# Selective scan stage: softplus, output and down products spread over the states, and GpSimd makes the product with C for three of the sixteen states from rows in SBUF

## The chip, the core and the metric

One core of a Trainium2 chip runs the whole program in one launch. The metric is device time in microseconds (us). The kernel before took 1541.23 us (median of 3 runs, 1536.33 to 1543.85).

## The reference, cut to what matters

A tokenizer (convolutions, a wavelet packet transform, layer norm) turns 32 images into 49 tokens each; with a class token and 32 text tokens that is a sequence of S = 82 rows of D = 192 for each of the 32 images. Then come a layer norm and a Mamba block with a gated FFN, then self-attention, then a routed feed-forward layer with 8 experts, two of them for each token. The change lies in the Mamba block alone:

```
xdbl = z @ W_xproj.T;  dt_in, Bm, Cm = split(xdbl, [96, 112])
dt   = softplus(dt_in @ W_dt.T + b_dt)          # (S, 384)
A    = -exp(A_log)                              # (384, 16)
h_t  = exp(dt_t * A) * h_(t-1) + (dt_t * z_t) * Bm_t     # for each of 16 states
y    = sum over states of h * Cm  + D_skip * z
x1   = x + y @ W_out.T;   out = x1 + FFN(rmsnorm(x1))
```

## The kernel before, in words

The block works in 8 rounds of G = 4 images, so N = 4 * 82 = 328 columns; the 384 inner channels are NI = 3 tiles of 128 partitions, and a tile of one state is 128 x 984. Within a round the code steps through the 16 states. Every engine runs the same skeleton in program order, `turn(i, par, s)`: its part of the scan for state s (`step`), a piece of the round behind (`post`, round i-1: output product, RMS norm, gated FFN, down product, sum into H) and a piece of the round ahead (`pre`, round i+1: transposes, gate and input products, x projection, softplus). TensorE and ScalarE do `post` and `pre` first and `step` last (`side_first`), VectorE and GpSimd do `step` first. Rounds 1 to 6 have all three parts, round 0 has no `post`, round 7 no `pre`.

What each engine does for one state:

- GpSimd: Bx = dtz * B (`inputs`), three states ahead, ring of 4.
- ScalarE: the decays exp(dt * A) into PSUM (`decays`), two states ahead in program order, but each half waits until the scan of the state before has read that half of the bank.
- VectorE: the scan in two halves (`scan`), from PSUM and Bx into hs, ring of 4; then the product hs * C in place (line 1230).
- TensorE: `spread_c`, a matmul with a one-hot matrix that spreads the C row of a state over 128 partitions of PSUM, two banks in turn; and `add_y`, two f32 matmuls with the identity that add the product to y in PSUM. The round's y is read from PSUM by VectorE (`drain`) in state 0 of the next round.

All products of `pre` and `post` share two PSUM banks (6 and 7) in turn. The list `SIDE_TILES` fixes that order, and `free(name)` makes TensorE wait until the tile two places earlier has been read; for RT1 that tile is O1, which is free once VectorE has made the second half of x1:

```
SIDE_TILES = [("O0", 0, s_x1, 2, 1), ("O1", 0, s_x1, 2, 2), ("RT0", 1, s_hT, 2, 1), ("RT1", 1, s_hT, 2, 2),
              ("RG0", 1, s_z, 3, 1), ("RI0", 1, s_z, 3, 1), ("RG1", 1, s_z, 3, 2), ("RI1", 1, s_z, 3, 2),
              ...
```

Places in the round: state 1, products O0 and O1 and both halves of x1 on VectorE; state 2, transposes RT0, RT1 and on ScalarE hT; states 3 to 5, gate and input products RGm, RIm, tanh on ScalarE, z on VectorE; state 6, x projection, the copy Bs of the B rows, which SyncE writes to DRAM and reads back spread over 128 partitions (Bb); state 7, the remainder terms of C in bf16; states 8 to 10, softplus; states 10 to 13, the FFN products and `th`, `av` on VectorE; state 14, down products N0, N1 and both halves of H.

Softplus is max(x,0) + log(1+exp(-|x|)), plus a rounding term of 1+u. ScalarE makes rl = relu, ax = abs, u = exp(-ax), ax = 1+u, lnw = Ln(1+u), ax = ax-1; GpSimd makes ax = u-ax, ax += lnw, dt = rl+ax (state 10) and dtz = dt*z (state 11).

## Time and profile before

| | us |
|---|---|
| median of 3 runs | 1541.23 |
| the profiled execution, its own time | 1542.03 |
| its span, first to last instruction | 1540.2 |
| TensorE busy, of the span | 1253.2 |
| VectorE | 1045.4 |
| ScalarE | 708.6 |
| GpSimd | 755.4 |
| scan stage, first scan to last product with C | 303.1 to 839.3 |

PE is TensorE, PEld its weight loads, DVE VectorE, ACT ScalarE, POOL GpSimd, SP SyncE. Busy time alone doesn't say what a change is worth. In this kernel the reader looks at one round of some 70 us, sees which engine has idle time there, and what ended it (in brackets at the end of a timeline row: idle time before it, and the instruction waited for).

### The profile page before, as it was taken

To read this page: it belongs to the slowest core of one execution; us is meant where nothing else is said; L and a number is where in the kernel's file an instruction comes from. 1 tells how busy PE (TensorE), PEld (TensorE's weight loads), DVE (VectorE), ACT (ScalarE), POOL (GpSimd) and SP (SyncE) were. 2 spreads that over 40 slices of the span, in tenths; PEclk is the share of its full clock that TensorE was granted. 3 is DMA by queue.
4 is the path that set the end of the run, shared out by engine and by line. 5 is a ranking of instruction groups with operands and counts; after the bars stand their busy time and mean duration, and the time that the engine had idled before them with its cause. 6 is when DMAs were issued, how large, how long until landed. Compare 5 with 4: busy or idle time off the path is not lost. (4 is left out here: it accounts for less than half of the span.)

```text
span 1540.2 us, 19619 instructions
## 1 busy us (share of the span) xinstructions
PE 1253.2 (81%) x5818; PEld 829.1 (54%) x5819; DVE 1045.4 (68%) x1960; ACT 708.6 (46%) x1486; POOL 755.4 (49%) x492
## 2 busy tenths in 40 slices
PE   6796746297898989898878899888898259999996
PEld 4342323143455545555444678777777237777775
DVE  3699787899888989789898566776766403333332
ACT  1147522576757677585853345443432012222221
POOL 2028963568767686757775301333345712222222
PEclk9697657699999999999999999997987569999998
DMA  5100100440404033040500011121211112222221
GB/s 161 53 1 0 28 8 27 154 137 9 132 1 132 30 101 107 25 131 0 154 7 0 2 48 48 50 64 49 67 26 25 40 47 38 35 37 37 35 37 21
DMA packets 71130, 80.89 MB, mean 53 GB/s; under 512 B 13231, under 2 KB 62918, under 8 KB 70970
## 3 DMA queue, kind: packets, MB, share of 16 engines
q1 hardware_dynamic: 51778, 68.50, 14.2%
q0 software_dynamic: 17152, 9.24, 4.4%
q10 hardware_dynamic: 2136, 2.37, 0.5%
q8 instruction: 32, 0.52, 0.1%
q14 instruction: 32, 0.25, 0.1%
HBM read 48.74 MB, written 30.01 MB: 51 GB/s over the span
## 5 line engine op out<-in xcount | busy, mean ns | idle before, releaser
L1333 POOL TENSOR_TENSOR Bx<-dtz,Bb 128x984 f32<-128x984 f32 x128 | 288.9, 2278 | 53.9 <-DVE hs L1220 53.9
L1220 DVE TENSOR_TENSOR_SCAN hs<-ps,Bx 128x492 f32<-128x492 f32 x256 | 287.6, 1164 | 30.4 <-ACT ps L1094 25.4
L1094 ACT ACTIVATE ps<-dt,A 128x324 f32<-128x324 f32 (+1 forms) x512 | 214.1, 454 | 106.3 <-DVE hs L1220 104.8
L954 PE MATMUL ps<-hs,b_id 128*128 128x492 f32 x512 | 243.4, 598 | 11.6 <-DVE y L1188 9.1
L2046 POOL DMA_INDIRECT out<-yt,dest x48 | 74.1, 1543 | 222.2 <-DVE yt L2033 216.8
L1230 DVE TENSOR_TENSOR hs<-hs,ps 128x984 f32<-128x984 f32 x128 | 150.2, 1174 | 2.6
L954 PEld LDWEIGHTS ps<-hs,b_id 128*128 128x128 f32 x512 | 94.3, 197 | 87.7 <-issue 82.3
L1927 PE MATMUL e_ps<-W,xT 97*128 (+1 forms) x384 | 139.9, 507 | 1.8 <-ACT xT L1981 1.0
L2019 DVE COPY hT__9516<-e_ps 128x768 f32<-128x768 f32 x48 | 46.0, 957 | 132.2 <-PE e_ps L1936 131.8
L1946 PE MATMUL e_ps<-W,hT__9516 128*128 x576 | 109.2, 327 | 0.8 <-DVE yb L2027 0.8
L1831 POOL TENSOR_TENSOR c_x<-c_x,bro 82x192 f32<-82x192 f32 x32 | 19.7, 614 | 182.2 <-DVE c_x L1677 181.7
L1987 ACT ACTIVATE hb<-e_ps 128x768 f32<-128x768 f32 x48 | 38.9, 811 | 145.7 <-PE e_ps L1927 145.7
L1822 POOL DMA_INDIRECT buckets<-XS,c_slot x64 | 91.2, 1425 | 24.9 <-issue 19.1
L1927 PEld LDWEIGHTS e_ps<-W,xT 97*128 97x128 f32 (+1 forms) x384 | 70.6, 194 | 56.1 <-issue 18.8
L920 PE MATMUL ps<-hfT,wug 96*128 96x328 f32 x256 | 80.7, 461 | 22.9 <-DVE av L1205 22.1
L1946 PEld LDWEIGHTS e_ps<-W,hT__9516 128*128 128x128 f32 x576 | 91.4, 190 | 1.4 <-issue 1.4
L492 POOL TENSOR_TENSOR DF<-DF,prod 96x441 f32<-96x441 f32 x84 | 87.6, 1043 | 6.6
L939 PE MATMUL ps<-P,sel 96*128 96x328 bf16 x128 | 40.2, 316 | 54.7 <-DVE hs L1230 40.9
L920 PEld LDWEIGHTS ps<-hfT,wug 96*128 96x128 f32 x256 | 48.3, 195 | 59.8 <-DVE av L1205 36.6
L1564 PEld LDWEIGHTS ps<-V,PT 82*82 82x82 f32 x768 | 69.0, 169 | 13.8 <-issue 7.6
L1981 ACT ACTIVATE xT<-e_ps,vec 96x128 f32<-96x128 f32 x96 | 38.5, 451 | 81.6 <-PE e_ps L1917 81.5
L1644 DVE TENSOR_REDUCE mx<-ps 82x12 f32<-82x984 f32 x32 | 37.7, 1177 | 54.1 <-PE ps L1551 53.9
(251 smaller groups left out, 2436.3 us busy)
## 6 DMA issues: line engine op xcount, KB each, us to landing
Bb<-b_rows SPq DMA_DIRECT2D x32, 656.0 KB, 6.7
buckets<-b_zero SPq DMA_DIRECT2D x8, 2288.0 KB, 15.3
xg<-buckets SPq DMA_DIRECT2D x48, 104.0 KB
xc<-in_xcol SPq DMA_DIRECT2D x4, 1176.0 KB, 9.1
W<-in_w1d SPq DMA_DIRECT2D x8, 582.0 KB
W<-in_w2d SPq DMA_DIRECT2D x8, 576.0 KB
out<-H SPq DMA_DIRECT2D x8, 246.0 KB
H<-P SPq DMA_DIRECT2D x4, 294.0 KB
```

The source lines that it names most:

```text
L492: g.tensor_tensor(out, a, prod[:, (9 * n + t) % PRODUCTS], ALU.add).then_inc(s_sum, 1)
L920: mm = pe.matmul(ps[:, wide(name, p), 0:N], wug[:, k, w_, m * 128:(m + 1) * 128], hfT[:, k, :], start=k == 0, stop=k == 1)
L954: mm = pe.matmul(ps[:, BANK_Y + h, 0:HALF], ident[:], f2(hs[:, s % LONG])[:, h * HALF:(h + 1) * HALF], start=s == 0, stop=s == STATE - 1)
L1094: a = act.activation(ps[:, BANK_A + h, c:c + w].rearrange("p (g t) -> p g t", t=S)[:, :, 1:S], dt[:, (par + t // STATE) % 2, m, g0 * S:g1 ...
L1220: v.tensor_tensor_scan(f2(hs[:, t % LONG])[:, c], ps[:, BANK_A + h, 0:HALF], f2(Bx[:, t % RING])[:, c], 0.0, ALU.mult, ALU.add).then_inc(s ...
L1230: v.tensor_tensor(hs[:, s % LONG], hs[:, s % LONG], ps[:, BANK_C + s % 2, 0:N].rearrange("p (a n) -> p a n", a=1).broadcast_to([128, NI, N ...
L1333: g.tensor_tensor(Bx[:, t % RING], dtz[:, p], Bb[:, p, t % STATE, :].rearrange("p (a n) -> p a n", a=1).broadcast_to([128, NI, N]), ALU.mu ...
L1564: mm = pe.matmul(ps[0:S, HEAD_OUT + c % 2, h * (DH + 1):(h + 1) * (DH + 1)], PT[:, c % 2, h, :], V[:, vpar, c, h, :], start=True, stop=True)
L1822: g.indirect_dma_start(out=xs, out_offset=bass.IndirectOffsetOnAxis(ap=slot[:, par, k, c:c + 1], axis=0), in_=XS[:, par, c, :], in_offset= ...
L1927: mm = pe.matmul(ps[:, 1 + 2 * p + h, 0:384], xT[c_, p, k, :], W1[c_, k, bass.ds(e, 1), h * 384:(h + 1) * 384].rearrange("p a n -> p (a n) ...
L1946: mm = pe.matmul(ps[:, 7, 0:D], hT[:, p, k, :], W2[:, k, bass.ds(e, 1), :].rearrange("p a n -> p (a n)"), start=k == 0, stop=k == KF - 1)
L2046: g.indirect_dma_start(out=out, out_offset=bass.IndirectOffsetOnAxis(ap=dest[:, p:p + 1], axis=0), in_=yt[:, p, :], in_offset=None, comput ...
```

## The change: what it does

1. States 1, 3 and 5 are POOLED. For them TensorE makes no `spread_c`, VectorE makes no product with C, and GpSimd multiplies hs by a row of C that lies in SBUF spread over 128 partitions (Cb, 3 x 328). GpSimd does it first thing in the state, ahead of the Bx three states on.
2. Bs holds the 16 C rows too (32 rows), and one more DMA per round loads Cb from DRAM. It waits until the products of the round before have read Cb.
3. TensorE puts `add_y` of a POOLED state off to the next state: in state 2 it adds states 1 and 2, and so on. Its `step` is empty in states 1, 3 and 5.
4. The output product is split: O0 in state 1, O1 in state 2, and x1 on VectorE likewise.
5. The down product is split: N0 in state 14, N1 in state 15, and H likewise.
6. ScalarE makes Ln in state 11 and no longer between the two copies of state 10; GpSimd adds it in state 11. The relu goes straight into dt. The rows xl are made in state 14 instead of 12.

```diff
+        POOLED = (1, 3, 5)
+        SPREAD = [s for s in range(STATE) if s not in POOLED]
+        NP_, NS_ = len(POOLED), len(SPREAD)
...
+                if j > 0:
+                    sp.wait_ge(s_hp, j * NP_)
+                sp.dma_start(Cb[:], b_d[par, STATE + POOLED[0]:STATE + POOLED[-1] + 1:2, :].rearrange("(a s) n -> a s n", a=1)
+                             .broadcast_to([128, NP_, N])).then_inc(s_Cb, 16)
...
             def post(p, par, s, other):          # TensorE
-                if s == 1:
-                    pe.wait_ge(s_y, p + 1)
-                    for h in range(2):
-                        free(f"O{h}", p, other)
...
+                if s in (1, 2):
+                    h = s - 1
+                    if h == 0:
+                        pe.wait_ge(s_y, p + 1)
+                    free(f"O{h}", p, other)
...
-                if s == 14:
-                    pe.wait_ge(s_av, p * 4 + 4)
-                    for h in range(2):
...
+                if s in (14, 15):
+                    h = s - 14
+                    if h == 0:
+                        pe.wait_ge(s_av, p * 4 + 4)
...
             def step(i, par, s, last):           # TensorE
-                if not last or s + 2 < STATE:
-                    spread_c(i, par, s + 2)
+                if s in POOLED:
+                    return
+                n = SPREAD.index(s)
+                if not last or n + 2 < NS_:
+                    spread_c(i, par, n + 2)
+                if s - 1 in POOLED:
+                    add_y(i, s - 1)
                 add_y(i, s)
...
                 if s == 10:                      # ScalarE
                     act.wait_ge(s_u, j + 1)
                     act.activation(f2(ax[:]), f2(u[:]), ACT.Copy, bias=1.0).then_inc(s_w1, 1)
-                    act.activation(f2(lnw[:]), f2(u[:]), ACT.Ln, bias=1.0)
-                    act.wait_ge(s_w1, j + 1)
-                    act.activation(f2(ax[:]), f2(ax[:]), ACT.Copy, bias=-1.0).then_inc(s_c1, 1)
-                if s == 12:
+                    act.wait_ge(s_w1, j * 2 + 1)
+                    act.activation(f2(ax[:]), f2(ax[:]), ACT.Copy, bias=-1.0).then_inc(s_w1, 1)
+                if s == 11:
+                    act.activation(f2(lnw[:]), f2(u[:]), ACT.Ln, bias=1.0).then_inc(s_c1, 1)
+                if s == 14:
...
             def post(p, par, s, other):          # VectorE
-                if s == 1:
-                    v.wait_ge(s_xl, (p + 1) * G)
-                    for h in range(2):
-                        v.wait_ge(s_o, p * 2 + (h + 1))
...
+                if s in (1, 2):
+                    h = s - 1
+                    if h == 0:
+                        v.wait_ge(s_xl, (p + 1) * G)
+                    v.wait_ge(s_o, p * 2 + (h + 1))
...
             def step(i, par, s, last):           # VectorE
-                v.wait_ge(s_scan, 2 * (i * STATE + s) + 2)
-                v.wait_ge(s_pc, i * STATE + (s + 1))
-                v.tensor_tensor(hs[:, s % LONG], hs[:, s % LONG],
...
+                if s not in POOLED:
+                    n = SPREAD.index(s)
+                    v.wait_ge(s_scan, 2 * (i * STATE + s) + 2)
...
+            def times_c(i, s):                   # GpSimd
+                c = POOLED.index(s)
+                if c == 0:
+                    g.wait_ge(s_Cb, i * 16 + 16)
+                g.wait_ge(s_scan, 2 * (i * STATE + s) + 2)
+                g.tensor_tensor(hs[:, s % LONG], hs[:, s % LONG],
+                                Cb[:, c, :].rearrange("p (a n) -> p a n", a=1).broadcast_to([128, NI, N]), ALU.mult).then_inc(s_hp, 1)
+
             def step(i, par, s, last):
+                if s in POOLED:
+                    times_c(i, s)
                 if not last or s + AHEAD < STATE:
                     inputs(i, par, s + AHEAD)
```

TensorE's order in states 1 and 2 of a round in the steady loop, before the change, from the output product O1 (wo) on: the spread of C (sel), the addition of state 1 to y (two matmuls, b_id with 128x492), the transposes RT0 and RT1 of hn, the next spread, the addition of state 2. REGISTER_ALU and ISA rows compute the values that waits need.

```order
L904 MATMUL ps<-wo,y 82x192 x6
L551 REGISTER_ALU
L939 MATMUL ps<-P_119,sel 128x328
L954 MATMUL ps<-hs,b_id 128x492 x2
L868 REGISTER_ALU
L851 ISA
L858 MATMUL ps<-b_id,hn 96x82 x4
L851 REGISTER_ALU
L858 MATMUL ps<-b_id,hn 96x82 x4
L551 REGISTER_ALU
L939 MATMUL ps<-P_119,sel 128x328
L954 MATMUL ps<-hs,b_id 128x492 x2
```

And with the change:

```order
L915 MATMUL ps<-wo,y 82x192 x6
L878 REGISTER_ALU
L861 ISA
L868 MATMUL ps<-b_id,hn 96x82 x4
L861 REGISTER_ALU
L868 MATMUL ps<-b_id,hn 96x82 x4
L551 REGISTER_ALU
L951 MATMUL ps<-P_119,sel 128x328
L969 MATMUL ps<-hs,b_id 128x492 x4
L884 ISA
L861 REGISTER_ALU
L888 MATMUL ps<-hT,wzg 128x328 x4
```

The spread and the addition that stood between O1 and the transposes are gone from there; the additions of states 1 and 2 (four matmuls) now stand together behind the transposes, ahead of the first gate product (L888, wzg).

VectorE in the same stretch before, from the first half of x1 (state 1) on; L1220 is half a scan, L1230 the product with C:

```order
L1197 TENSOR_TENSOR x_133<-xl,ps 82x384
L1196 REGISTER_ALU
L1197 TENSOR_TENSOR x_133<-xl,ps 82x384
L1230 TENSOR_TENSOR hs<-hs,ps 128x984
L1215 ISA
L1217 REGISTER_ALU
L1220 SCALAR_TENSOR_TENSOR hs<-ps,Bx 128x492
L1215 REGISTER_ALU
L1220 SCALAR_TENSOR_TENSOR hs<-ps,Bx 128x492
L1230 TENSOR_TENSOR hs<-hs,ps 128x984
```

And with the change, from the scan of state 3 to the first z (L1192):

```order
L1246 SCALAR_TENSOR_TENSOR hs<-ps,Bx 128x492
L1241 REGISTER_ALU
L1246 SCALAR_TENSOR_TENSOR hs<-ps,Bx 128x492
L1221 REGISTER_ALU
L1222 TENSOR_TENSOR x_133<-xl,ps 82x384
L1241 ISA
L1243 REGISTER_ALU
L1246 SCALAR_TENSOR_TENSOR hs<-ps,Bx 128x492
L1241 REGISTER_ALU
L1246 SCALAR_TENSOR_TENSOR hs<-ps,Bx 128x492
L1190 ISA
L1192 SCALAR_TENSOR_TENSOR z<-sg,ps 128x328
```

The second half of x1 (x_133) moved from behind the scan of state 2 to behind the scan of state 3, and is followed by the scan of state 4 with no product in between.

ScalarE in state 10 and at the start of state 11 before, with Ln (lnw) between the copies and the decays of state 12 (L1094) behind it:

```order
L1084 ACTIVATE th<-ps 128x328
L1051 ACTIVATE ax<-u 128x984
L1052 ACT_TABLE_LOAD
L1052 ACTIVATE lnw<-u 128x984
L1054 ACTIVATE ax<-ax 128x984
L551 ISA
L1094 ACT_TABLE_LOAD
L1094 ACTIVATE ps<-dt,A 128x4x81
L1094 ACTIVATE ps<-dt,A 128x2x81 x2
L1094 ACTIVATE ps<-dt,A 128x4x81
L1083 REGISTER_ALU
L1084 ACTIVATE th<-ps 128x328
```

And with the change:

```order
L1076 ACTIVATE ax<-ax 128x984
L551 ISA
L1118 ACTIVATE ps<-dt,A 128x4x81
L1118 ACTIVATE ps<-dt,A 128x2x81 x2
L1118 ACTIVATE ps<-dt,A 128x4x81
L1107 REGISTER_ALU
L1108 ACTIVATE th<-ps 128x328
L1078 ACT_TABLE_LOAD
L1078 ACTIVATE lnw<-u 128x984
L551 ISA
L1118 ACT_TABLE_LOAD
L1118 ACTIVATE ps<-dt,A 128x4x81
```

The decays of state 12 (L1118) now stand ahead of the tanh of state 11 and of Ln (L1078), and it is the decays of state 13 that stand behind the two table loads.

## Rows read from the trace of the kernel before

**Rows 1.** The page: busy time of the engines, all of the span.

```profile
PE 1253.2 (81%) x5818; PEld 829.1 (54%) x5819; DVE 1045.4 (68%) x1960; ACT 708.6 (46%) x1486; POOL 755.4 (49%) x492
```

**Rows 2.** Timeline of DVE: start us, us, line, tiles, count, idle before.

```profile
366.94 1.60 DVE L1188 SCALAR_TENSOR_TENSOR y<-z,vec,ps 128x328 f32<-128x328 f32 x4
...
575.00 1.61 DVE L1188 SCALAR_TENSOR_TENSOR y<-z,vec,ps 128x328 f32<-128x328 f32 x4
...
609.27 1.18 DVE L1230 TENSOR_TENSOR hs<-hs,ps 128x984 f32<-128x984 f32 x1
...
653.95 0.55 DVE L1197 TENSOR_TENSOR x<-xl,ps 82x384 f32<-82x384 f32 x1 [1.40 <-PE ps L904]
654.42 1.17 DVE L1230 TENSOR_TENSOR hs<-hs,ps 128x984 f32<-128x984 f32 x1
655.51 2.24 DVE L1220 TENSOR_TENSOR_SCAN hs<-ps,Bx 128x492 f32<-128x492 f32 x2
...
692.49 2.25 DVE L1220 TENSOR_TENSOR_SCAN hs<-ps,Bx 128x492 f32<-128x492 f32 x2 [3.12 <-ACT ps L1094]
...
709.69 0.55 DVE L1210 TENSOR_TENSOR H<-x,ps 82x384 f32 x1 [1.98 <-PE ps L931]
...
782.98 1.61 DVE L1188 SCALAR_TENSOR_TENSOR y<-z,vec,ps 128x328 f32<-128x328 f32 x4
...
841.29 1.61 DVE L1188 SCALAR_TENSOR_TENSOR y<-z,vec,ps 128x328 f32<-128x328 f32 x4 [2.01 <-PE ps L954]
```

**Rows 3.** One round in a window: us, busy us and count of each engine, PEclk, DMA.

```profile
644.70:715.00 70.30, 62.83 (x227) 36.43 (x227) 62.01 (x70) 48.80 (x115) 49.05 (x25) 0.98 0.22 72
```

**Rows 4.** Timeline of PE in the same round.

```profile
646.43 3.40 PE L954 MATMUL ps<-hs,b_id 128*128 128x492 f32 x4 [1.30 <-DVE y L1188]
649.63 4.28 PE L904 MATMUL ps<-wo,y 128*82 128x192 f32 x24
...
655.54 0.73 PE L858 MATMUL ps<-b_id,hn 82*96 82x82 f32 x8
656.11 0.30 PE L939 MATMUL ps<-P,sel 96*128 96x328 bf16 x1
656.25 1.81 PE L954 MATMUL ps<-hs,b_id 128*128 128x492 f32 x4
657.90 2.37 PE L878 MATMUL ps<-hT,wzg 96*128 96x328 f32 x8
...
680.27 0.72 PE L864 MATMUL ps<-dtin,wdt 96*128 96x328 f32 x2
...
695.71 2.47 PE L920 MATMUL ps<-hfT,wug 96*128 96x328 f32 x8 [3.11 <-DVE av L1205]
```

**Rows 5.** Windows: PEclk (third last number) after a short idle of PE.

```profile
646.40:649.60 3.20, 3.17 (x4) 1.22 (x5) 3.17 (x4) 1.70 (x4) 1.07 (x1) 0.54 0.00 0
649.60:680.90 31.30, 31.30 (x123) 18.94 (x121) 28.43 (x31) 21.62 (x58) 18.83 (x12) 0.99 0.17 58
```

**Rows 6.** The page: groups of instructions, count, busy us, mean ns of one.

```profile
L1333 POOL TENSOR_TENSOR Bx<-dtz,Bb 128x984 f32<-128x984 f32 x128 | 288.9, 2278 | 53.9 <-DVE hs L1220 53.9
L1230 DVE TENSOR_TENSOR hs<-hs,ps 128x984 f32<-128x984 f32 x128 | 150.2, 1174 | 2.6
```

**Rows 7.** Timeline of ACT: hT of state 2, then Ln and the decays behind it.

```profile
656.03 0.95 ACT L1025 ACTIVATE hT<-ps,vec 96x328 f32<-96x328 f32 x2 [3.32 <-PE ps L858]
...
686.90 1.28 ACT L1052 ACT_TABLE_LOAD   x1
688.20 1.02 ACT L1052 ACTIVATE lnw<-u 128x984 f32<-128x984 f32 x1
...
690.15 1.28 ACT L1094 ACT_TABLE_LOAD   x1
691.45 1.63 ACT L1094 ACTIVATE ps<-dt,A 128x324 f32<-128x324 f32 x4
```

**Rows 8.** DMA issues: count, KB each, median us from issue to landing.

```profile
Bb<-b_rows SPq DMA_DIRECT2D x32, 656.0 KB, 6.7
```

More of the change, by code:

```diff
@@ L771, in turn @@
                     step(i, par, s, last)
-                if has_post and not (last and s == 14):
+                if has_post and not (last and s >= 14):
                     post(i - 1, 1 - par, s, None if last else i + 1)
@@ L829, in _ @@
             sp.wait_ge(s_P3, ROUNDS)
+            sp.wait_ge(s_Cb, 16 * ROUNDS)
+            sp.wait_ge(s_hp, NP_ * ROUNDS)
             fr.loads(sp)
@@ L974, in ending @@
                 post(last - 1, 0, 14, None)
+                post(last - 1, 0, 15, None)
                 post(last, 1, 1, None)
+                post(last, 1, 2, None)
                 fr.turn(pe)
@@ L991, in ending @@
                 post(last, 1, 14, None)
+                post(last, 1, 15, None)
                 pe.wait_ge(fr.s_qT, 3)
@@ L1278, in ending @@
                 post(last, 1, 14, None)
+                post(last, 1, 15, None)
                 v.wait_ge(s_H, 2 * ROUNDS + 2)
```

112 lines of the change are left out of this document (61 added, 51 removed).

## The prediction

> **What bounds the kernel now.** I read the page first: VectorE is busy 1045 us of the span, more than any engine but TensorE [rows 1], and in the scan stage both are nearly full. The stage's unit is the round: six rounds with all their parts lie between the drains at 366.94 and 782.98, so a round takes 416.04 / 6 = 69.34 us [rows 2]. In the window of one round VectorE is busy 62.0 of 70.3 us and TensorE 62.8, while ScalarE and GpSimd have some 49 [rows 3]. VectorE's timeline says where its other 8 us go: 3.12 us ahead of the scan of state 12, for decays; 1.98 us for the second half of the down product; 1.40 us for the second output product, in this round alone; the rest are pieces near 0.5 us [rows 2]. TensorE's timeline is the one that decides this case. From y in state 0 (646.43) to the last step-size matmul (680.27) it has no idle time: the window 649.60 to 680.90 shows 31.30 us busy of 31.30 [rows 4, 5]. In states 1 to 9 VectorE and TensorE are level. In states 10 to 0 both have gaps.
>
> The granted clock of TensorE drops at times. [...]
>
> **The change, part by part.** *Products.* VectorE loses three products in a round, each 1.09 us from start to start (654.42 to 655.51) [rows 2]: 3.3 us a round, 26 us in all if they were on the path throughout. GpSimd gains three; the trace has none, but Bx is the same form and size, 2278 ns against VectorE's 1174 [rows 6], so I take 2.27 us, 6.8 a round, beside 21 us idle [rows 3]. Over states 1 to 6 GpSimd has for two states two Bx and one product, 6.8 us; VectorE has two scans (4.35), one product and side work of 0.4 to 0.5 us each, 6.3. Bx is made three states ahead, so this is hidden where side work is, and about level where it isn't (last round, below).
>
> *The x1 chain.* All three states lie in 1 to 6, where TensorE has no slack, and there the change adds order. I walk the round from the start of the drain, at full clock, with the durations of [rows 4, 7]: an addition 1.65 us from start to start (1.81 less what the next one overlaps), a spread 0.15, a pair of gate and input products 2.2, four transposes 0.28, hT 0.45 each half, decays 0.8 per half. Before, the walk puts the product of state 9 at 34.2 us; the trace has 609.27 - 575.00 = 34.27 [rows 2].
> After: y at 1.7 us; addition of state 0, O0 and O1 to 7.5; RT0 to 7.75. RT1 needs O1's bank, which the second half of x1 frees. That stands behind the scan of state 3, done at 9.6, so x1 ends at 10.1 and TensorE idles 2.4 us. hT's second half ends at 11.2, the decays of state 4 behind it on ScalarE allow that scan at 12.1 where VectorE was ready at 10.1: wait 2.0. TensorE does the additions of states 1 and 2 and a spread (3.45) ahead of RG0, and RI0 is done at 16.2; VectorE has been at z since 14.3: wait 2.1. z frees the bank for RG1, RI1; the additions of states 3 and 4 follow (to 22.6), then RG2, RI2 to 24.8, with VectorE at the third z from 22.6: wait 2.4. The x projection and the additions of 5 and 6 push hfT and with it the decays of state 9: wait 1.6. The product of state 9 lands at 37.6. So the first half is 3.4 us longer, with 3.3 us of products gone: TensorE's work is shorter by three spreads alone (0.45), and it gains idle time of 2.4 and twice 0.7.
>
> *Ln.* Before, ScalarE does copy, table load, Ln, copy, table load ahead of the decays of state 12: wait 3.12 us [rows 2, 7]. After, state 12's decays go first and those of state 13 stand behind load, Ln, load: 1.28 + 1.02 + 1.28 + 0.8 us, of which VectorE's scan, th, av and product cover all but 1.0. Gain 2.1. *Down product in halves.* The wait of 1.98 [rows 2] shrinks to 0.4, as the first half runs beside the scan of state 15: gain 1.5. *Output in halves.* Its gain, 1.40 in one round in two at most, is in the walk. Second half, from the product of state 9: 33.7 to 30.3, so -3.4.
>
> *At nothing:* the wider Bs (same columns); relu into dt and the third add (same sizes); xl in state 14 (read in state 1 of the next round). The load of Cb is 3/4 of a Bb group, which lands in 6.7 us [rows 8]; it is issued in state 7 and wanted in state 1 of the next round, some 40 us on. Without that cover it would cost its 7 us.
>
> **Sum,** against the profiled execution's own 1542.03 us, 0.8 above the median. Middle rounds: 67.95 to 68.03 in the walk, so 0. First round: I take -0.7, between 0 and -3.3. Last round (58.31 from 782.98 to 841.29 [rows 2]): no gate products there, so the x1 chain costs nothing, but with little side work GpSimd's product in state 5 makes the scan of state 7 wait 1.8, and the walk gives -1.9 of the possible -3.3. Clock: before, the walk is 69.34 - 67.95 = 1.4 us a round short of the trace; that is what the low stretches cost. After, the idle time in state 0 stays and there is a new one of 2.4 us ahead of RT1; a low stretch over one addition costs 1.65 us [rows 4], over two 3.3, now on the path of all that follows. Nothing lost to the clock gives 68.0, both stretches in each round 71.3. I take 69.9, +0.55 in six rounds: +3.3. In all -0.7 - 1.9 + 3.3 = +0.7, against the median **1542 us**.
>
> [...]
>
> **Rivals.** *Full gain:* VectorE alone is the bound, and the round loses 3.3 for the products and 3.4 behind, 6.7 x 6, plus 4 = 44 us, 1497; half of it 1520. For it: VectorE's busy share. Against it: TensorE without idle time in just those states, and RT1's wait. 10 in 100 (1497 to 1524). *No low clock:* the walk holds and neither stretch drops: -1.35 x 6 - 2.6 = -11, 1530. 15 in 100. *Low clock in both places each round* (the other side; it decides from about one added low stretch in each round): 71.3 - 69.34 = 2.0, x 6, less 2.6, +9, 1551. For it: TensorE's idle time grows just where it is on the path. Against: the walk leaves most of the idle time of state 11 out. 24 in 100. *GpSimd becomes the bound:* its product holds up Bx three on; the scan of state 7 waits 1.8 us in all eight rounds on top, +12, 1554. For it: 6.8 against 6.3 us per pair. Against: three states' lead. 6 in 100.
>
> **How the numbers follow.** The forecast has the remaining 45 in 100. A measurement of this kernel can't tell less than 0.5% (7.7 us) from no change. The likeliest case has 1535 to 1549. The range reaches to no low clock below and to the first slower rivals above: **1526 to 1556**. Faster by over 0.5%: full gain 10, no low clock 13 of 15, so 0.23; slower: 24 and 6, less 1, so 0.29; same 0.48.
>
> **What would show it.** In the trace after, a middle round from drain to drain near 69 to 70 us; in it VectorE waits of about 2 us at the scan of state 4 (for decays), at the first z and at the third z, 1.0 us at the scan of state 13 and none at 12, 0.4 at H. TensorE idles some 2.4 us between RT0 and RT1. GpSimd's products 2.27 us. The prediction is wrong if z is not waited for (then full gain), if the clock in states 0 to 4 is near 1.00 throughout, or if scans wait for Bx in the middle rounds.

## The result, and the profile after

The changed kernel took 1559.3 us (median of 4 runs, 1557.01 to 1559.88), the kernel before on the same chip 1538.8: ratio 1.0122, 95% interval 1.0102 to 1.0141. The forecast was 1542 and no change, with 1526 to 1556; the kernel became 1.2% slower and landed above the range. The profiled execution after has a span of 1557.1 us and took 1558.94, so it is 16.9 us longer in span than the one before. Ratios compare each kernel with the kernel before on its own chip; the microseconds of kernels that ran on different chips are compared less exactly (the kernel before had medians of 1538.8 to 1542.8).

The page after, engines and the two groups of GpSimd's products [rows 1, 6]:

```profile
PE 1259.6 (81%) x5794; PEld 831.5 (53%) x5795; DVE 1019.0 (65%) x1936; ACT 708.7 (46%) x1486; POOL 807.4 (52%) x516
...
L1365 POOL TENSOR_TENSOR Bx<-dtz,Bb 128x984 f32<-128x984 f32 x128 | 288.5, 2277 | 0.0
...
L1380 POOL TENSOR_TENSOR hs<-hs,Cb 128x984 f32<-128x984 f32 x24 | 54.4, 2266 | 44.7 <-DVE hs L1246 44.7
```

VectorE lost 26.4 us of busy time and GpSimd gained 52. The 24 products with C take 2266 ns, as forecast. The time is nonetheless longer, so the gain went into waits. VectorE's timeline of one round, the rows that carry a wait and the drains (columns as in [rows 2]):

```profile
585.94 1.61 DVE L1212 SCALAR_TENSOR_TENSOR y<-z,vec,ps 128x328 f32<-128x328 f32 x4
...
598.16 2.25 DVE L1246 TENSOR_TENSOR_SCAN hs<-ps,Bx 128x492 f32<-128x492 f32 x2 [2.04 <-ACT ps L1118]
604.13 0.50 DVE L1192 SCALAR_TENSOR_TENSOR z<-sg,ps 128x328 f32<-128x328 f32 x1 [3.71 <-PE ps L888]
...
612.92 0.50 DVE L1192 SCALAR_TENSOR_TENSOR z<-sg,ps 128x328 f32<-128x328 f32 x1 [2.48 <-PE ps L888]
...
618.49 2.25 DVE L1246 TENSOR_TENSOR_SCAN hs<-ps,Bx 128x492 f32<-128x492 f32 x2 [0.35 <-ACT ps L1118]
...
623.71 2.25 DVE L1246 TENSOR_TENSOR_SCAN hs<-ps,Bx 128x492 f32<-128x492 f32 x2 [1.67 <-ACT ps L1118]
...
640.41 2.25 DVE L1246 TENSOR_TENSOR_SCAN hs<-ps,Bx 128x492 f32<-128x492 f32 x2 [1.33 <-POOL Bx L1365]
...
655.25 0.55 DVE L1236 TENSOR_TENSOR H<-x,ps 82x384 f32 x1 [0.52 <-PE ps L943]
658.55 1.18 DVE L1258 TENSOR_TENSOR hs<-hs,ps 128x984 f32<-128x984 f32 x1 [2.76 <-issue]
659.65 0.55 DVE L1212 SCALAR_TENSOR_TENSOR y<-z,vec,ps 128x328 f32<-128x328 f32 x1
```

The walk is the prediction's step through one round, instruction by instruction. Each wait that it forecast is there: 2.04 at the scan of state 4, a wait at the first z and at the third (2.48), 1.67 at the scan of state 9, 1.33 at the scan of state 13 and none at 12, 0.52 at H. Two waits are not as forecast. The first z waits 3.71 instead of 2.1, and the first product behind the turn of the loop (658.55) waits 2.76 us for nothing that the profile shows ("issue"). TensorE's timeline says why z is late:

```profile
587.70 1.89 PE L969 MATMUL ps<-hs,b_id 128*128 128x492 f32 x4 [1.43 <-DVE y L1212]
589.42 4.06 PE L915 MATMUL ps<-wo,y 128*82 128x192 f32 x24
593.32 0.45 PE L868 MATMUL ps<-b_id,hn 82*96 82x82 f32 x4
596.18 0.49 PE L868 MATMUL ps<-b_id,hn 82*96 82x82 f32 x4 [2.41 <-DVE x L1222]
...
596.65 5.16 PE L969 MATMUL ps<-hs,b_id 128*128 128x492 f32 x8
601.65 2.37 PE L888 MATMUL ps<-hT,wzg 96*128 96x328 f32 x8
604.69 2.47 PE L888 MATMUL ps<-hT,wzg 96*128 96x328 f32 x8 [0.67 <-DVE z L1192]
...
607.14 3.46 PE L969 MATMUL ps<-hs,b_id 128*128 128x492 f32 x8
```

Behind the idle 2.41 us ahead of RT1 the paired addition of states 1 and 2 takes 5.16 us; the same eight matmuls for states 3 and 4 take 3.46. The windows of the whole round, of the slow pair's inside and of the other pair (third last number: granted clock) show that it is the clock, 0.54 in the slow pair against 1.00 in the other:

```profile
585.90:659.60 73.70, 62.78 (x223) 36.21 (x223) 58.27 (x65) 49.06 (x115) 55.35 (x27) 0.98 0.23 76
596.70:600.20 3.50, 3.50 (x6) 1.49 (x6) 2.04 (x2) 2.77 (x9) 3.50 (x2) 0.54 0.00 0
607.20:610.60 3.40, 3.40 (x10) 1.62 (x9) 3.24 (x4) 2.77 (x8) 2.63 (x2) 1.00 0.00 0
```

From drain to drain the seven rounds after read, in us (the loop's body is two rounds, and it turns at the ends of the second and the fourth):

| kernel | round 1 | 2 | 3 | 4 | 5 | 6 | mean | 7 |
|---|---|---|---|---|---|---|---|---|
| before [rows 2] | 69.67 | 70.04 | 68.35 | 69.67 | 70.05 | 68.26 | 69.34 | 58.31 |
| after | 72.37 | 71.89 | 72.30 | 73.71 | 72.63 | 70.99 | 72.31 | 56.29 |

So six rounds lost 17.9 us; the stretch from the first scan to the first drain lost 1.3, the last round gained 2.0, and outside the scan stage the two differ by 0.3: together the 16.9 us of span.

### The profile page after: what moved, and what is told of

It is laid out like the page before. It is cut to its first block and busy times, and to the rows that moved or that the text cites. A ratio compares the mean times of both kernels' runs of the same rounds, so it can differ in the third digit from the quotient of the medians.

```text
span 1557.1 us, 19581 instructions
## 1 busy us (share of the span) xinstructions
PE 1259.6 (81%) x5794; PEld 831.5 (53%) x5795; DVE 1019.0 (65%) x1936; ACT 708.7 (46%) x1486; POOL 807.4 (52%) x516
## 5 line engine op out<-in xcount | busy, mean ns | idle before, releaser
L1118 ACT ACTIVATE ps<-dt,A 128x324 f32<-128x324 f32 (+1 forms) x512 | 212.4, 454 | 73.6 <-DVE hs L1246 73.4
L969 PEld LDWEIGHTS ps<-hs,b_id 128*128 128x128 f32 x512 | 97.8, 202 | 103.4 <-issue 95.5
L1258 DVE TENSOR_TENSOR hs<-hs,ps 128x984 f32<-128x984 f32 x104 | 122.0, 1173 | 8.3 <-issue 5.4
L1969 PEld LDWEIGHTS e_ps<-W,xT 97*128 97x128 f32 (+1 forms) x384 | 69.9, 192 | 55.1 <-issue 17.1
L1380 POOL TENSOR_TENSOR hs<-hs,Cb 128x984 f32<-128x984 f32 x24 | 54.4, 2266 | 44.7 <-DVE hs L1246 44.7
L1593 PE MATMUL ps<-kB,qT 128*82 128x328 f32 (+1 forms) x256 | 70.7, 427 | 3.1 <-DVE E L1690 2.0
```

The source lines that it names most:

```text
L969: mm = pe.matmul(ps[:, BANK_Y + h, 0:HALF], ident[:], f2(hs[:, s % LONG])[:, h * HALF:(h + 1) * HALF], start=s == 0, stop=s == STATE - 1)
L1118: a = act.activation(ps[:, BANK_A + h, c:c + w].rearrange("p (g t) -> p g t", t=S)[:, :, 1:S], dt[:, (par + t // STATE) % 2, m, g0 * S:g1 ...
L1258: v.tensor_tensor(hs[:, s % LONG], hs[:, s % LONG], ps[:, BANK_C + (par * NS_ + n) % 2, 0:N].rearrange("p (a n) -> p a n", a=1).broadcast_ ...
L1593: mm = pe.matmul(ps[0:S, SCORES + h0 // 6, (h0 % 6) * S:(h0 % 6 + h1 - h0) * S], qT[:, par, m_, q * S:(q + 1) * S], kB[:, par, m_, q, j:j ...
L1969: mm = pe.matmul(ps[:, 1 + 2 * p + h, 0:384], xT[c_, p, k, :], W1[c_, k, bass.ds(e, 1), h * 384:(h + 1) * 384].rearrange("p a n -> p (a n) ...
```

## Experiments

Fifteen kernels ran, each with the kernel before on the same chip. The theories in their expectations: A, the order of TensorE's work (RT1 behind the second half of x1, additions in pairs ahead of the gate products, low clock behind the new idle time); B, GpSimd's 6.8 us of products hold up Bx; C, the second half of H in state 15 lays VectorE's turn of the loop bare; D and E, formed later, are two forms of C, which lay the wait at the turn to the code of VectorE's loop body: to its length (D), or to its place in the program (E).

| kernel | us | ratio to before (95%) | mean of rounds 1 to 6 |
|---|---|---|---|
| products alone | 1572.2 | 1.0200 (1.0160 to 1.0239) | 73.35 |
| output halves alone | 1560.3 | 1.0116 (1.0076 to 1.0157) | 71.99 |
| the whole change | 1559.3 | 1.0122 (1.0102 to 1.0141) | 72.31 |
| change, output whole | 1548.7 | 1.0049 (1.0032 to 1.0066) | 69.99 |
| Ln step alone | 1530.7 | 0.9928 (0.9901 to 0.9954) | 68.25 |
| Ln step and down halves alone | 1515.3 | 0.9823 (0.9785 to 0.9861) | 65.34 |

### One part at a time

*e1*: the change without its other steps: output and down products whole, Ln back between the copies (TensorE's part is shown; VectorE's x1 and H and ScalarE's Ln and xl go back likewise; the relu still goes into dt).

```diff
-                if s in (1, 2):
-                    h = s - 1
...
+                if s == 1:
+                    for h in range(2):
...
-                if s in (14, 15):
-                    h = s - 14
...
+                if s == 14:
+                    for h in range(2):
```

> The changed kernel with the output product whole in state 1, the down product whole in state 14 and Ln back in state 10: of the change only the three products with C on GpSimd stay, with their paired additions to y on TensorE. Theory A (the order of TensorE's work: RT1 behind the second half of x1, and the additions of two states ahead of the gate products, with low clock behind the new idle time): the paired additions alone already make VectorE wait at the first and third z, so no gain from three products less; a middle round of 70 to 72 us against 69.3, in all 1540 to 1556, no wait of the scan of state 4 for hT. Theory B (GpSimd's extra 6.8 us a round holds up Bx): scans wait for Bx in the middle rounds, 1555 or more. Theory C (VectorE's turn of the loop laid bare by the second half of H in state 15): without that half here no wait of 2.6 us at the loop's turn; says nothing of the rest, by it alone the kernel would be 26 us faster, 1515.

*e3*: the change with O0, O1 and x1 whole in state 1 (the first of the two edits above), all else kept.

> The changed kernel with the output product and x1 whole in state 1 again, all else as changed. Theory A: RT1 has no wait of 2.4 us, the scan of state 4 none of 2.0, the first z waits less, and less of the round runs at low clock; a middle round of 67.5 to 69.5 us, in all 1528 to 1540. Theory B: no change from the changed kernel, 1559. Theory C: the two waits of 2.6 us at the loop's turn stay, 5 us of the loss.

*e4*: the kernel before with only items 5 and 6 of the change (down halves; Ln in state 11, relu into dt, xl in state 14):

```diff
-                act.activation(rl[:, m, :], ps[:, bank(f"D{m}"), 0:N], ACT.Relu, bias=vec[:, V_B_DT + m:V_B_DT + m + 1])
+                act.activation(dt[:, par, m, :], ps[:, bank(f"D{m}"), 0:N], ACT.Relu, bias=vec[:, V_B_DT + m:V_B_DT + m + 1])
...
-                    act.activation(f2(lnw[:]), f2(u[:]), ACT.Ln, bias=1.0)
...
+                if s == 11:
+                    act.activation(f2(lnw[:]), f2(u[:]), ACT.Ln, bias=1.0).then_inc(s_c1, 1)
```

> The kernel before with Ln moved to state 11 (relu into dt, xl in state 14) and the down product in two halves, nothing else. Theory A: both only take waits away in the second half of the round, where both engines have gaps: 3.5 us a round by the walk, 2.1 for Ln and 1.5 for the down product, so 65 to 66 us for a middle round and 1512 to 1522 in all. Theory C: of this 5 us are given back at the loop's turn, 1520. Rival that these gains are taken by the next wait: 1538.

*e9*: the kernel before with only item 4 (output in halves), as its diff ahead of the prediction has it:

```diff
-                if s == 1:
+                if s in (1, 2):
+                    h = s - 1
```

> The kernel before with the output product and x1 in two halves in states 1 and 2, nothing else. Theory A: RT1 waits for the second half of x1, now behind the scan of state 3, hT and the gate products are late by 2 to 3 us, and the clock falls more often: a middle round of 70 to 71.5 us, 1544 to 1554 in all. Rival (the halves alone do no harm, the loss comes with the additions in pairs): 1536 to 1541.

Measured: e1 1572.2, e3 1548.7, e4 1515.3 and e9 1560.3 us. The change has a good half and a bad half. Items 5 and 6 gain 27 us; the products then cost 33 (1515.3 to 1548.7), and the output in halves another 11 (18 when alone). Only e4 lies in the range that theory A gave it (1512 to 1522). The three with a loss lie 6 to 16 us above A's ranges, and e1 lies in B's (1555 or more), so at this point B was not excluded. In e1's trace no scan of rounds 1 to 6 waits for Bx; as forecast z waits (1.6 and 2.5 us) and no wait shows at the turn. More than A had allowed for is the low clock, in state 0 of rounds 2, 4 and 6 (additions of 3.49 to 3.52 us, at a granted clock of 0.53 and 0.54) and in the FFN products of the other three (4.74 us at 0.50 for eight matmuls that take 2.47 at 1.00 in rounds 2, 4 and 6). VectorE's waits in a round of e4 are few, columns as before:

```profile
654.77 0.49 DVE L1177 TENSOR_TENSOR R<-ps,P 64x328 f32<-64x328 f32 x1 [0.50 <-ACT P L1038]
656.92 2.25 DVE L1225 TENSOR_TENSOR_SCAN hs<-ps,Bx 128x492 f32<-128x492 f32 x2 [0.57 <-ACT ps L1098]
...
677.02 2.25 DVE L1225 TENSOR_TENSOR_SCAN hs<-ps,Bx 128x492 f32<-128x492 f32 x2 [1.33 <-ACT ps L1098]
...
691.85 0.55 DVE L1215 TENSOR_TENSOR H<-x,ps 82x384 f32 x1 [0.52 <-PE ps L932]
```

In e9, whose products are all on VectorE, TensorE's addition in state 0 takes 3.39 us at 586.54 (clock 0.55), and the five other rounds after the first show 3.3 to 3.6 there. Theory A's wait is there only in part: RT1 waits 0.36 us, since the late addition has used up the time in which it would have waited, and VectorE then waits 0.95 at the scan of state 4 and 0.2 to 0.4 at each z. A second low stretch lies in state 12 of each round: at 636.20 eight FFN matmuls take 3.64 us at a clock of 0.66, where the eight before them take 2.47, and the first half of H waits 0.75 for it. So e9's 18 us are for a good part the clock, and why it is low in so many of its rounds isn't shown.

### Why the products cost 33 us

*e10*: e4, in which TensorE alone puts the additions of states 1, 3 and 5 off to the next state. GpSimd makes no product.

```diff
                     spread_c(i, par, s + 2)
+                if s in (1, 3, 5):
+                    return
+                if s - 1 in (1, 3, 5):
+                    add_y(i, s - 1)
                 add_y(i, s)
```

> The version with only the Ln step moved and the down product in halves (1515 us, 65.3 us a middle round), plus one thing of the change: TensorE puts the addition to y of states 1, 3 and 5 off to the next state, so that two additions stand together ahead of the gate products. Spreads of C and all products stay where they are, on VectorE; GpSimd gets nothing. Theory A (order of TensorE's work): z waits again at RG0 and RG1, about 1.6 and 2.4 us, the middle round grows by 2.3 to 3.3 us, total 1529 to 1536, half or more of the 33 us that lie between 1515 and the version with products and all but the output in halves (1549). Theory B (GpSimd's extra work): nothing changes, 1513 to 1518. Theory D (the loop body of VectorE and the others has outgrown what is at hand when it turns): nothing changes either, the counts of instructions are the same, 1513 to 1518.

*e11*: e4, in which GpSimd alone gets a product more in states 1, 3 and 5, of the same form and size, into a free tile. It adds work that the reference doesn't have.

```diff
             def step(i, par, s, last):           # GpSimd
+                if s in (1, 3, 5):
+                    g.wait_ge(s_scan, 2 * (i * STATE + s) + 2)
+                    g.tensor_tensor(rl[:], dtz[:, par], Bb[:, par, s, :]..., ALU.mult)
```

> The same version of 1515 us, plus GpSimd's extra load alone: in states 1, 3 and 5 GpSimd makes one more product of 128x984 after the scan, from rows of B in SBUF into a free tile, ahead of its Bx, and nobody waits for it. VectorE keeps its products, so this computes nothing new and takes nothing away. Theory A: Bx is made three states ahead, so the middle round stays within 0.5 us of 65.3; total 1513 to 1520. Theory B: scans of states 4 to 8 wait for Bx, about 1 to 2 us a round, 1523 to 1545; if it holds all of the 33 us, 1549. Theory D: nothing, 1513 to 1520.

*e7*: e3 with the late additions one at a time: 0, 2, 1, 4, 3, then 5 and 6. VectorE's wait for a free place in the ring of hs, which counts additions, is fitted to the new order (not shown).

```diff
             def step(i, par, s, last):           # TensorE
+                if s - 2 in POOLED:
+                    add_y(i, s - 2)
...
-                if s - 1 in POOLED:
+                if s - 1 == POOLED[-1]:
                     add_y(i, s - 1)
```

> The changed kernel with the output product and x1 whole in state 1 again (1549 us, 70.0 us a middle round), and TensorE's additions spread out: states 1, 3 and 5 are added later and one at a time, in the order 0, 2, 1, 4, 3, 5, 6, so that no two additions stand together ahead of a gate product. Products stay on GpSimd. Theory A: the waits of z (1.6 and 2.5 us) shrink below 1 us each and the middle round comes down to 66 to 67.5, total 1525 to 1535. Theory B: scans still wait for Bx and the round stays at 69.5 to 70, 1545 to 1551. Theory D: the wait of some 2.6 us ahead of the first instruction of VectorE's loop body stays in its rounds whatever the order, and if it is what keeps this from 1515, the round is 1 to 2 us above the walk's 65.4.

*e8*: e7 with the down product and H whole in state 14 (the second of e1's edits).

> The one before (additions one at a time) with the down product and H whole in state 14 again. The wait of H for its second half comes back (2.0 us in place of 0.5), and nothing of the round behind stands between the scan of state 15 and the turn of the loop. Theory A: the round grows by 1.4 us, total 8 us above the one before. Theory D (instructions of the longer loop body have to be brought in at each turn, 2.6 us laid bare when H stands last, hidden when it doesn't): the wait at the turn goes, the round is the same or up to 1 us shorter, total within 6 us of the one before on either side.

Measured: e10 1535.7 us (0.998, 0.9956 to 1.0003), e11 1514.4 (0.9836, 0.9807 to 0.9865), e7 1537.8 (0.9971, 0.9949 to 0.9994), e8 1545.0 (1.0033, 1.0007 to 1.0060). B falls: the page of e11 shows GpSimd's 24 extra products, and the time is that of e4.

```profile
L1342 POOL TENSOR_TENSOR Bx<-dtz,Bb 128x984 f32<-128x984 f32 x128 | 288.9, 2283 | 0.0
...
L1357 POOL TENSOR_TENSOR rl<-dtz,Bb 128x984 f32<-128x984 f32 x24 | 54.6, 2273 | 37.6 <-DVE hs L1226 37.6
```

A holds for 20 of the 33 us, in its range (1529 to 1536), but its waits at z are shorter than the 1.6 and 2.4 that it forecast. They are back with no product moved at all; a pair of additions takes 3.46 us at a clock of 1.00 ahead of RG0:

```profile
587.84 0.49 DVE L1176 SCALAR_TENSOR_TENSOR z<-sg,ps 128x328 f32<-128x328 f32 x1 [0.45 <-PE ps L878]
...
596.62 0.50 DVE L1176 SCALAR_TENSOR_TENSOR z<-sg,ps 128x328 f32<-128x328 f32 x1 [1.39 <-PE ps L878]
```

The round grows from 65.34 to 68.14 us. What moving the products does by itself shows when e3 is set beside e10. The rounds with no low clock and no turn are 67.83 to 67.95 us in e10 and 68.00 in e3 (its sixth), though VectorE has three products less there. In e3 each of the two waits at z is longer by 1.1 us, which is the product that VectorE no longer makes ahead of it:

```profile
732.00 0.49 DVE L1190 SCALAR_TENSOR_TENSOR z<-sg,ps 128x328 f32<-128x328 f32 x1 [1.57 <-PE ps L888]
...
740.78 0.50 DVE L1190 SCALAR_TENSOR_TENSOR z<-sg,ps 128x328 f32<-128x328 f32 x1 [2.48 <-PE ps L888]
```

In its six rounds e3 takes 11.1 us more than e10. Of these 5.3 are waits at the turn of the loop (2.67 and 2.60); most of the rest is low clock in state 0 of rounds 1, 3 and 5 (additions of 3.36, 3.62 and 2.99 us at a clock of 0.56, 0.50 and 0.61, against 1.89 us at 1.00).

e7 came out above A's 1525 to 1535, because of the turn of the loop. Its rounds are 66.12, 68.94, 69.35, 68.67, 68.57, 66.12: the first and the last show what its order is worth, the four beside the two turns are 2.5 to 3.2 us longer, for a wait of 2.85 and 2.57 us at "issue" and a low clock of TensorE behind it (0.50 in state 0). In e8 no "issue" wait stands at the turn, as theory D had it, and H waits 1.98 again; that the scan ahead of the turn covers the wait is inferred. e8's 1545.0 lies 7 us above e7, past D's 6 and near A's 8, so its time doesn't decide between the two, and its trace does.

e8 also prices the low clock by itself. TensorE's state 0 in the second round and in the third, with the same idle time ahead of it:

```profile
434.88 1.89 PE L967 MATMUL ps<-hs,b_id 128*128 128x492 f32 x4 [1.30 <-DVE y L1209]
...
436.61 4.06 PE L914 MATMUL ps<-wo,y 128*82 128x192 f32 x24
...
502.58 3.62 PE L967 MATMUL ps<-hs,b_id 128*128 128x492 f32 x4 [1.32 <-DVE y L1209]
...
505.99 5.36 PE L914 MATMUL ps<-wo,y 128*82 128x192 f32 x24
```

Addition and output product add up to 5.95 us in the one and 8.98 in the other, at a granted clock of 1.00 and 0.66. Rounds 1 and 2 are 67.68 us both, round 3 is 70.68 with no other wait that they lack: a low stretch over both is worth 3.0 us of a round. The rounds behind the two turns, 3 and 5, have an addition of 3.62 us in e7 and e8 alike; e8 has low stretches in rounds 4 and 6 too (3.41 and 3.53). Why the clock falls after the same 1.3 us of idle time in one round and not in another I can't say.

### The turn of the loop, and Ln alone

*e12*: e7, where the semaphore of the spreads counts states, so that VectorE's wait reuses a register; *e13*: the whole change with the same edit.

```diff
-                          start=True, stop=True).then_inc(s_pc, 1)
+                          start=True, stop=True).then_inc(s_pc, SPREAD[n % NS_] - SPREAD[n % NS_ - 1] if n % NS_ else 1)
...
-                    v.wait_ge(s_pc, i * NS_ + (n + 1))
+                    v.wait_ge(s_pc, i * STATE + (s + 1))
```

> The version with products on GpSimd and TensorE's additions one at a time (1538 us), with one edit: the semaphore that counts the spreads of C counts states and no longer spreads, so that VectorE's wait for it reuses a value that it has in a register. VectorE's loop body falls from 285 to 261 rows (before the change 267); no operation on data changes. Theory D (a longer body has to be brought in again when the loop turns): the wait of 2.6 to 2.9 us for nothing that the profile shows goes from both turns, and with it the low clock of TensorE behind it; the rounds beside the turns come from 68.6 to 69.4 down to the 66.1 of the others, 1526 to 1530 in all. Rival (the wait at the turn belongs to GpSimd's products or to H in state 15, not to the code): nothing changes, 1535 to 1540.

> The whole change (1559 us) with the same edit to the counting semaphore: VectorE's loop body 261 rows in place of 285. Theory D: the two waits of 2.6 and 2.8 us at the turns go, with up to as much again in low clock behind them: 1547 to 1554. Rival: no change, 1557 to 1560. In neither case does it come near 1541, since the order of TensorE's work stays.

*e14*: e4 with idle instructions in VectorE's stream.

```diff
             def step(i, par, s, last):           # VectorE
+                if 1 <= s <= 10:
+                    v.sem_inc(s_pad, 1)
```

> The version of 1515 us with ten more instructions a round in VectorE's stream, twenty in the loop body, which only count up a semaphore that nobody waits for. GpSimd makes no product, TensorE's order is that of 1515. Theory D: the wait for nothing at the two turns appears here too, 2.6 us each and perhaps low clock behind it, total 1521 to 1528. Rival (it is not the length of the code): what twenty short instructions cost themselves, at most 1 us a round, the same in every round: 1515 to 1521, and no round at a turn longer than the others.

*e5*: the kernel before with item 6 alone, the edit shown at e4.

> The kernel before with the Ln step alone moved to state 11 (relu straight into dt, rows xl in state 14); down product whole. The prediction took 2.1 us a round for it, so 12.6 in six rounds and 1526 to 1530. If that term is right and the term of 1.5 us a round for the down product too, the two together give 21 of the 26 us that both together gained (1515); the rest would be low clock of TensorE in state 0, which two of six rounds show before and none with both. A gain of under 8 us (over 1533) would say that the down product, or what its halves do to TensorE's idle time, brings more than its term.

Measured: e12 1532.1 us (0.9944, 0.9928 to 0.9959), e13 1556.5 (1.0100, 1.0065 to 1.0136), e14 1513.5 (0.9819, 0.9786 to 0.9852), e5 1530.7. D falls: e14 is longer and doesn't wait, and e12 and e13 still wait 2.6 to 2.8 us at both turns. Their edit also proved empty for VectorE: what it saves in register instructions comes back as separate waits, and VectorE's compiled program has as many instructions as before it (3183 in the traces of e7, e12, e13 and after alike). TensorE executes 23 more. In the compiled program the loop body is 344 instructions before the change (585 to 928) and 332 after it (579 to 910): the change made it shorter. Their times are 3 to 6 us less than those of e7 and the whole change, but the intervals of the ratios overlap (0.9928 to 0.9959 and 0.9949 to 0.9994; 1.0065 to 1.0136 and 1.0102 to 1.0141), so this isn't clear of noise. Both fell between the ranges of D (1526 to 1530, 1547 to 1554) and its rival (1535 to 1540, 1557 to 1560).

e5 puts the Ln step at 11 us, just short of the 1526 to 1530 expected. Its trace has the forecast wait gone, but the additions in state 0 at 3.10 us, at a clock of 0.59, in every round, and so x1 late by 1.40:

```profile
579.20 0.55 DVE L1198 TENSOR_TENSOR x<-xl,ps 82x384 f32<-82x384 f32 x1 [1.40 <-PE ps L904]
...
620.13 2.25 DVE L1221 TENSOR_TENSOR_SCAN hs<-ps,Bx 128x492 f32<-128x492 f32 x2 [1.33 <-POOL Bx L1335]
...
633.17 0.55 DVE L1211 TENSOR_TENSOR H<-x,ps 82x384 f32 x1 [1.98 <-PE ps L931]
```

The windows of the queues' own traffic show what is behind the turn. From 500 to 760 us the queue that brings instructions is silent before the change and in e4; after it:

```profile
q14 instruction: 9, 0.07, 0.1%
```

Three of these come at a turn, about 2.5 us apart (in e7 near 494.4, 497.0 and 499.6, around the product at 496.69), the others later in the body, five for each two rounds. Between the later ones VectorE goes through 126 and 135 instructions (499.6 to 554.5 to 609.8), so the packets keep step with its program. On the whole span the page counts 32 before, 31 in e4, e5 and e14, and 41 in each kernel with the products so far, at about 8 KB each (0.34 MB for the 41). That led to Theory E: what counts is not the length of VectorE's body but its place in the program, and with the body moved back packets and wait go.

### The place of the loop body

*e15* is e7 and *e17* the whole change, each with ten idle instructions ahead of the loop:

```diff
             def first():                         # VectorE
                 v.sem_inc(s_left, 1)
+                for _ in range(10):
+                    v.sem_inc(s_pad, 1)
```

*e16* is e14 with fifteen idle instructions a round:

```diff
-                if 1 <= s <= 10:
+                if 1 <= s <= 15:
```

> The version with products on GpSimd and TensorE's additions one at a time (1538 us), plus ten instructions that count up an unused semaphore in VectorE's stream before its first round, outside the loop. The loop body keeps its 332 instructions (before the change 344) but stands ten later in the program: 589 to 920 in place of 579 to 910, inside the stretch 585 to 928 that the body had before. [...]

> The version of 1515 us with fifteen in place of ten idle instructions a round in VectorE's stream; with ten (body 595 to 958 in VectorE's program) it had no wait at the turn and 1513 us. Now the body is 600 to 973. [...] Rival (position and length don't matter at this size): 1512 to 1518, no packets in the loop.

> The whole change (1559 us) with the same ten instructions before VectorE's first round. Theory E: the two waits of 2.6 and 2.8 us go, 1551 to 1555, and what then remains above the kernel before (1541) is the order of TensorE's work and its clock alone: 10 to 14 us, so the change is slower without the turn too. Rivals: no change, 1556 to 1560.

Measured: e15 1521.0 us (0.9865, 0.9840 to 0.9889), e16 1525.0 (0.9894, 0.9869 to 0.9919), e17 1549.6 (1.0052, 1.0032 to 1.0071). Theory E had given 1526 to 1531, 1520 to 1527 and 1551 to 1555: e16 is in its range, and e15 and e17 are a little below theirs, further from the rivals. The same turn in e7, e15 and e16, each from the second half of H to the first product of the next body:

```profile
493.29 0.55 DVE L1235 TENSOR_TENSOR H<-x,ps 82x384 f32 x1 [0.52 <-PE ps L942]
496.69 1.18 DVE L1257 TENSOR_TENSOR hs<-hs,ps 128x984 f32<-128x984 f32 x1 [2.85 <-issue]
```

```profile
495.09 0.55 DVE L1235 TENSOR_TENSOR H<-x,ps 82x384 f32 x1 [0.52 <-PE ps L942]
495.78 1.18 DVE L1259 TENSOR_TENSOR hs<-hs,ps 128x984 f32<-128x984 f32 x1
```

```profile
493.39 0.55 DVE L1215 TENSOR_TENSOR H<-x,ps 82x384 f32 x1 [0.52 <-PE ps L932]
496.57 1.18 DVE L1237 TENSOR_TENSOR hs<-hs,ps 128x984 f32<-128x984 f32 x1 [2.63 <-issue]
```

Ten instructions before the loop take the wait away; five more a round than in e14 bring it into a kernel that has no product on GpSimd. The page's instruction packets follow: e15 31, e17 32, e16 41 against 31 in e14.

The places are my count in the compiled programs. The traces bear out the lengths: between the third drain and the fifth VectorE has 342 instructions before, 331 after and 330, 362 and 373 in e15, e14 and e16.

| VectorE's loop body | first to last instruction | packets on the page | wait at the turns |
|---|---|---|---|
| before, e4 | 585 to 928 | 32, 31 | none |
| e14 | 595 to 958 | 31 | none |
| e15, e17 | 589 to 920 | 31, 32 | none |
| after, e7 | 579 to 910 | 41 | 2.6 to 2.9 |
| e16 | 600 to 973 | 41 | 2.6, 2.8 |

The bodies that lie between 585 and 958, of 332 to 364 instructions, have neither packets nor a wait at the turns; the one that begins at 579 and the one that ends at 973 have five packets for each two rounds, and the wait. e7 and e15 differ in the place alone, their bodies being equally long; e16 has the longest body too, so it doesn't tell place from length by itself. Its range was worked out from the rows above it and from the 126 and 135 instructions between two packets in e7, and was an estimate. Where the limits lie between 579 and 585 and between 958 and 973, what sets them, and why it is five packets, isn't shown. e1, e3, e8, e12 and e13 have 41 packets too; in e1 and e8, whose H is whole in state 14, no wait shows with them. A rival had the length of GpSimd's or SyncE's body bring packets and wait, and gave e15 1532 to 1539. GpSimd's body is longer in e11 (115 instructions between two drains two rounds apart) than after the change (111), and e11 has 31 packets; SyncE's is as long in e15 as in e7 (18). So neither is the cause.

## Why the prediction was wrong, point by point

*Products, GpSimd's side: right.* 2266 ns each, and hidden: e11.

*The x1 chain: right in each place, a little short in its sum.* The wait of 2.41 ahead of RT1, 2.04 at the scan of state 4, 2.48 at the third z and 1.67 at the scan of state 9 were forecast at 2.4, 2.0, 2.4 and 1.6. The sum can be read in round 5 of e17, the one round of the whole change with neither low clock nor turn:

```profile
666.13 2.25 DVE L1246 TENSOR_TENSOR_SCAN hs<-ps,Bx 128x492 f32<-128x492 f32 x2 [2.04 <-ACT ps L1118]
...
670.39 0.50 DVE L1192 SCALAR_TENSOR_TENSOR z<-sg,ps 128x328 f32<-128x328 f32 x1 [2.01 <-PE ps L888]
...
679.18 0.50 DVE L1192 SCALAR_TENSOR_TENSOR z<-sg,ps 128x328 f32<-128x328 f32 x1 [2.48 <-PE ps L888]
...
684.75 2.26 DVE L1246 TENSOR_TENSOR_SCAN hs<-ps,Bx 128x492 f32<-128x492 f32 x2 [0.35 <-ACT ps L1118]
...
689.97 2.25 DVE L1246 TENSOR_TENSOR_SCAN hs<-ps,Bx 128x492 f32<-128x492 f32 x2 [1.67 <-ACT ps L1118]
...
706.80 2.25 DVE L1246 TENSOR_TENSOR_SCAN hs<-ps,Bx 128x492 f32<-128x492 f32 x2 [1.46 <-POOL Bx L1367]
...
721.64 0.55 DVE L1236 TENSOR_TENSOR H<-x,ps 82x384 f32 x1 [0.52 <-PE ps L943]
```

These waits add up to 10.5 us. Round 3 of before, equally undisturbed (68.35), has 0.50, 0.57, 3.12 and 1.98, or 6.2. So 4.4 us of waits came for 3.3 us of products, and that round takes 69.42: 1.07 more, where "Middle rounds: 67.95 to 68.03 in the walk, so 0" had 0.08. The walk missed 0.35 at the scan of state 8 and took 1.0 for the 1.46 at that of state 13. Six rounds: 6.4 of the 17.9 us.

*Clock: the direction right, the size too small.* The step was "I take 69.9, +0.55 in six rounds". Measured against the undisturbed rounds, before lost 5.9 us to it in six rounds (1.0 a round, not 1.4), and after 17.4, less 5.4 of waits at the turns, 12.0 (2.0 a round). The difference is 6.1 us instead of 3.3. A single stretch cost what the prediction had taken for it, 1.65: 1.70 at the pair, 1.0 to 1.3 at x1. Its count was too low. The paired addition behind RT1's wait runs at the low level wholly or in part in five of the six rounds after (4.81 to 5.16 us at a clock of 0.67 to 0.72 against 3.46 at 1.00), and the addition in state 0 in three (3.06 to 3.45 at 0.53 to 0.59, against 1.89 at 1.00). One stretch of before that did not drop, the 2.47 us behind 3.11 us of idle time at 695.71 [rows 4], says little against such a count. The same place dropped in rounds 1 and 4 of that very trace, behind the same wait (at 624.34 it took 2.98 us, at a clock of 0.81, and here 3.13 us at 0.77):

```profile
416.28 3.13 PE L920 MATMUL ps<-hfT,wug 96*128 96x328 f32 x8 [3.11 <-DVE av L1205]
```

The rival of 71.3 us a round took both stretches, in state 0 and behind the 2.4 us ahead of RT1, as low in each round. For the second the rounds after bear it out in five of six. Part of the 6.1 belongs to the turn: the additions in state 0 of rounds 3 and 5, right behind it, are slow (3.31 and 3.45 us), and in e17 they take 1.89. The step fails without the turn too: against the undisturbed rounds e17 lost 11.2 us, 5.3 more than before and still above the 3.3, its first round alone 4.8. e17, with the turns out of the way, has a mean of 71.29 and 1549.6 us in all, the rival's 1551 nearly; but it gets there with 6.4 us of the walk's shortfall, so the rival is only half borne out: behind RT1's wait the pair is slow in five of its six rounds, in state 0 the addition in the first alone.

*The turn: not in the prediction at all.* 5.4 us of waits in the profile. Taking them away gives 6.1 us back in the rounds and 9.7 in the medians (1559.3 to 1549.6, ratios 1.0122 and 1.0052); in e7, where they also set off low clock in rounds 3 and 5, 16.8 (1537.8 to 1521.0), of which some 6 lie behind the scan stage in the one profile of each and are not explained. With 1549.6 the change is still slower by 0.5% (1.0032 to 1.0071), so the sign did not hang on the turn, but the range would have held. That VectorE waits there for instructions is an inference from the packets that come in at the same turns: the traces put the 2.6 to 2.9 us down to nothing, and in e1 and e8 the packets come without them.

*Ln, -2.1: 1.8.* The wait of 3.12 became 1.33 (e5). *Down in halves, -1.5: 1.46.* From 1.98 to 0.52. Together 3.3 us a round, 20 us. Of the rest of the 27 that e4 gained, some 4 are low clock, which e4 has in its first round only, and 2 lie ahead of the first drain. *First round, -0.7: +1.3* (in round 0 z already waits 3.49 and 2.48 us, a term 2.0 us off). *Last round, -1.9: -2.0.*

So the steps that failed are three terms of the sum, over six rounds: the walk 6.4 us (0.5 in the prediction, taken as 0), the clock 6.1 (3.3 in the prediction) and the turn 5.4 (no term). Together they are the 17.9 us.

*Where VectorE's 3.3 us went.* e15 answers it: with additions one at a time, no wait at the turn and additions in state 0 of 1.89 us throughout, its rounds after the first are 66.2 us against e4's 65.0. VectorE is busy 2.9 us less in a round (58.75 of 66.17 us against 61.66 of 65.08) and idle 4.0 us more. Scans wait 1.29 and 1.07 us for additions that came later (the ring of hs has four places) and x1 waits 1.09:

```profile
570.71 0.55 DVE L1221 TENSOR_TENSOR x<-xl,ps 82x384 f32<-82x384 f32 x1 [1.09 <-PE ps L914]
...
582.33 2.25 DVE L1245 TENSOR_TENSOR_SCAN hs<-ps,Bx 128x492 f32<-128x492 f32 x2 [1.29 <-PE ps L968]
...
591.30 2.25 DVE L1245 TENSOR_TENSOR_SCAN hs<-ps,Bx 128x492 f32<-128x492 f32 x2 [1.07 <-PE ps L968]
```

The work taken from VectorE was not what bound states 1 to 6; TensorE's order was, as e3 beside e10 shows too. The best kernel is therefore e4, the change without its products and without the output in halves: 1515.3 us, 0.9823 of before; e11 and e14 repeat it with harmless additions (1514.4, 1513.5).

## What to carry to other kernels

A change of several parts should be priced part by part: here two parts gained 27 us and two lost 44. Work moved off a busy engine was worth nothing here (e3 beside e10), in a stretch where another engine had no idle time, and the order that it forced on that engine (additions in pairs: 20 us) was paid for. In a kernel with a loop, look at the instruction packets inside it: if they come on each turn, moving the body by a few instructions, as cheap as ten idle ones ahead of the loop, was worth 10 to 17 us in 1550 here, and five idle instructions more a round lost some 12 (e14 to e16). And where a clock or a wait varies from round to round, read all rounds before arguing from one: the row at 695.71 of before had slow twins in rounds 1 and 4.
